# Four-layer mixture-of-experts kernel: gates of the first mixture broadcast by DMA, experts summed on GpSimd, routing steps in later places

## The reference, cut to what matters

```
# end of layer 1, dense mixture of 4 experts, every token goes through all four
gw  = softmax(h @ w_moe_gate.T)                # 4 gates of a token
hid = silu(h @ w1[e].T + b1[e])                # 128 -> 512, for each e
x   = x + sum_e gw[e] * (hid @ w2[e].T + b2[e])
# layer 2, one of 8 experts of a token
probs = softmax(layernorm(x) @ gate_w.T)
top   = max(probs); top_val = top / (top + 1e-8); expert = argmax(probs)
out   = layernorm(expert_ffn(...) * top_val)
```

## Time and profile before

| | |
|---|---|
| median of 3 runs | 1566.64 us |
| profiled execution | 1570.3 us, its span 1568.1 us |
| mixture stage, from its first instruction to the next stage's | about 474.5 to 958.2 us |
| PE / PEld busy | 84% / 65% of the span |
| DVE / ACT / POOL busy | 68% / 47% / 44% of the span |
| granted TensorE clock | 0.941 over the span |

### The profile page before, as it was taken

How to read it: one execution, slowest core, us unless ns; L and a number is a source line. 1 busy time by engine, 2 the same in 40 slices (tenths; PEclk the granted TensorE clock), 3 DMA queues, 4 the chain that set the end, 5 groups by cost and what they waited for, 6 DMA issues and landing times. The chain is left out here.

```text
span 1568.1 us, 33973 instructions
## 1 busy us (share of the span) xinstructions
PE 1310.5 (84%) x10546; PEld 1014.7 (65%) x10546; DVE 1063.9 (68%) x3597; ACT 743.8 (47%) x1503; POOL 694.1 (44%) x845
## 2 busy tenths in 40 slices
PE   3899999999875999999999964674787887829996
PEld 1566666666644888888888853564555655629996
DVE  3677777777646788888888863565588788722221
ACT  2345454545324676666666632453333333315553
POOL 2344444444320244545353542234366666525665
PEclk9899999999967999999999986998899999959998
DMA  2231212222102000000000004564211111259881
GB/s 79 29 41 26 36 27 33 29 31 31 17 1 81 3 14 8 14 7 14 7 12 9 11 11 123 167 178 118 72 52 46 46 51 45 40 189 312 261 266 40
DMA packets 61575, 100.97 MB, mean 64 GB/s; under 512 B 9698, under 2 KB 36331, under 8 KB 61120
## 3 DMA queue, kind: packets, MB, share of 16 engines
q1 hardware_dynamic: 51648, 78.58, 19.5%
q0 software_dynamic: 9856, 21.52, 4.4%
HBM read 62.96 MB, written 29.75 MB: 59 GB/s over the span
## 5 line engine op out<-in xcount | busy, mean ns | idle before, releaser
L1137 DVE TENSOR_TENSOR m_Sl<-m_S,m_Sh 128x512 fp32r<-128x512 f32 x256 | 174.8, 692 | 32.5 <-ACT m_S L1049 27.6
L1049 ACT ACTIVATE m_S<-PS,W 128x512 f32<-128x512 f32 x256 | 175.6, 686 | 33.4 <-PE PS L957 30.2
L1403 POOL DMA_INDIRECT rows<-r_row,r_posi x128 | 143.0, 1117 | 35.6 <-issue 35.6
L1389 POOL TENSOR_TENSOR r_soft<-r_euler,r_soft 128x32 f32<-128x32 f32 x16 | 86.9, 5429 | 132.5 <-DVE r_soft L1287 132.5
L1044 ACT ACTIVATE m_Sh<-PS,W 128x512 fp32r<-128x512 f32 x128 | 88.2, 689 | 106.2 <-PE PS L957 105.0
L750 DVE TENSOR_TENSOR am<-PS,C 128x512 f32<-128x512 f32 x192 | 119.4, 677 | 19.9 <-PE PS L442 19.9
L955 PE MATMUL PS<-m_HH,m_w1h 128*128 128x512 f32 x256 | 110.7, 432 | 14.5 <-DVE m_HL L1101 14.3
L1608 PEld LDWEIGHTS PS<-f_wt,f_hid 128*128 128x128 f32 x960 | 119.5, 192 | 4.2
L1608 PE MATMUL PS<-f_wt,f_hid 128*128 128x128 f32 x960 | 119.9, 275 | 0.0
L1597 PE MATMUL PS<-f_xT,f_wt 128*128 128x256 f32 x480 | 119.9, 387 | 0.0
L343 POOL TENSOR_TENSOR am<-am,C 128x512 f32<-128x512 f32 x64 | 81.4, 1272 | 80.2 <-ACT am L623 80.2
(11 more groups left out here) (242 smaller groups left out, 3242.5 us busy)
## 6 DMA issues: line engine op xcount, KB each, us to landing
f_wt<-wr SPq DMA_DIRECT2D x40, 578.0 KB
f_row<-rows SPq DMA_DIRECT2D x40, 260.0 KB
f_wt<-wr SPq DMA_DIRECT2D x40, 256.0 KB, 2.8
f_row<-rows SPq DMA_DIRECT2D x40, 132.0 KB, 2.1
mid<-f_res SPq DMA_DIRECT2D x40, 128.0 KB, 2.6
rows<-r_padding SPq DMA_DIRECT2D x16, 260.0 KB
X<-x SPq DMA_DIRECT2D x16, 256.0 KB, 5.5
qr<-qphi SPq DMA_DIRECT2D x64, 64.0 KB
```

Source lines behind the costliest of these rows:

```text
L1049: nc.scalar.activation(S[:, n % 3, :], PS[:, n % 3, :], ACT.Silu, bias=w("b1")[:, n:n + 1]).then_inc(s_ready, 1)
L1137: nc.vector.tensor_tensor(Sl[:, n % 4, :], S[:, n % 3, :], Sh[:, n % 4, :].bitcast(F32), ALU.subtract).then_inc(sl_ready, 1)
L1403: nc.gpsimd.indirect_dma_start(out=self.rows, out_offset=bass.IndirectOffsetOnAxis(ap=self.posi[:, u, t:t + 1], axis=0), in_=self.row[:, u ...
```

## The change

The gates are no longer spread over the partitions by PE. They are transposed once (2 transposes), written to a small DRAM tensor, and SP loads for each batch the 4 x 512 gates into all 128 partitions by one DMA with a repeated source (1 MB in SBUF), into one of two buffers. `gated` writes each expert to its own buffer (five in all), POOL adds them up in three 128x512 additions (`sums`), and PE transposes only the sum. `ROUNDED` becomes `(3,)`: ACT now writes `Sh` in three of four places. The first weights `w1` are loaded into `raw1` at the end of the front; weights are split one expert at a time, the high half on ACT, the low half on DVE, most of it inside batch 0. The router's steps of a batch move to the turn after, in other places, with two row buffers. Its exp becomes two Silus on ACT: e^y = -silu(y)/silu(-y). The count-dependent padding is issued half by SP and half by ACT, in the second router too. `sel` leaves the constants (256 KB).

```diff
@@ mixture, SP
-            sp.dma_start(raw1[:, :], w1t).then_inc(w1_in, 16)
-            sp.dma_start(raw2[:, :], w2t).then_inc(w2_in, 16)
+            for q in range(MOE):
+                sp.dma_start(raw2[:, q * SEQ:(q + 1) * SEQ], w2t[:, q * SEQ:(q + 1) * SEQ]).then_inc(w2_in[q], 16)
+            sp.wait_ge(gT_ready, 1)
+            sp.dma_start(gates_dram.rearrange("(h e) t p -> (e t) h p", h=2), gT[:, :, :]).then_inc(gates_out, 16)
+            sp.wait_ge(gates_out, 16)
+
+            def one(b, v, p, r, tp, tr):
+                if b is not None:
+                    if isinstance(b, int) and b == 1:
+                        sp.wait_ge(w_split, 2 * MOE)
+                    if not isinstance(b, int) or b >= 2:
+                        sp.wait_ge(oe_ready, MOE * (b + (-1)))
+                    src = gates_dram[:, bass.ds(b * CT, CT), :].rearrange("e t p -> e (t p)").unsqueeze(0)
+                    sp.dma_start(gb[v][:, :, :], src.to_broadcast([P, MOE, SEQ])).then_inc(gb_in[v], 16)
+            over_batches(sp, one)
             routing.sp_padding(sp)
@@ mixture, POOL
+            def sums(b, e, v):
+
+                pool.wait_ge(oe_ready, MOE * b + e + 1)
+                if e > 1:
+                    pool.wait_ge(summed, 3 * b + e - 1)
+                acc = oe[:, total_of(v), :]
+                nc.gpsimd.tensor_tensor(acc, acc, oe[:, e, :], ALU.add).then_inc(summed, 1)
+
+            def one(b, v, p, r, tp, tr):
+                if p is not None:
+                    sums(p, 2, 1 - v)
+                    sums(p, 3, 1 - v)
+                route(routing.pool_inverse_deviation, pool, p, 1 - v, tp)
+                if b is not None:
+                    sums(b, 1, v)
+                route(routing.pool_scatter, pool, r, v, tr)
@@ mixture, PE
+            def back(b, v):
+
+                pe.wait_ge(summed, 3 * b + 3)
+                after_previous(pe, x_ready, b)
                 for t in range(CT):
+                    mm = nc.tensor.transpose(PS[:, 7, t * P:(t + 1) * P], oe[:, total_of(v), t * P:(t + 1) * P], ident)
                 mm.then_inc(back_psum, 1)
...
                     lagging = chunk(b, p, n, 3)
                     if lagging:
                         down(*lagging)
+                    if n == 0:
+                        route(routing.pe_turn, pe, r, v, tr)
+                    if n == 3:
+                        route(routing.pe_scores, pe, r, v, tr)
+                    if n == 7 and p is not None:
+                        back(p, 1 - v)
+                    if n == 8:
+                        route(routing.pe_count, pe, r, v, tr)
@@ mixture, DVE
                     if n % 4 == 3:
                         lagging = chunk(b, p, n, 7)
                         if lagging:
+                            gated(lagging[0], lagging[1] // 4, v if n >= 7 else 1 - v)
+                    if n == 3:
+                        route(routing.dve_largest, dve, r, v, tr)
+                    if n == 4 and more:
+                        split_first(b + 1, 1 - v)
+                    if n == 5:
+                        route(routing.dve_pick, dve, r, v, tr)
+                    if n == 6 and more:
+                        split_second(b + 1, 1 - v)
+                    if n == 8 and p is not None:
+                        residual(p)
+                    if n == 9:
+                        route(routing.dve_statistics, dve, p, 1 - v, tp)
+                    if n == 10:
+                        route(routing.dve_place, dve, r, v, tr)
+                    if n == 12:
+                        route(routing.dve_gate, dve, r, v, tr)
+                    if n == 13:
+                        route(routing.dve_normalise, dve, p, 1 - v, tp)
@@ Routing
+    def act_exp(self, act, b, u, turn):
+
+        act.wait_ge(self.soft_ready, b + 1)
+        self.nc.scalar.activation(self.soft[:, 1, :, :], self.soft[:, 0, :, :], ACT.Silu)
+        self.nc.scalar.activation(self.soft[:, 2, :, :], self.soft[:, 0, :, :], ACT.Silu, scale=-1.0).then_inc(self.exp_ready, 1)
```

More of the change, by code:

```diff
@@ L942, in _ @@
         def _(pe):
-            pe.wait_ge(w_split, 3)
+            first = lambda b: isinstance(b, int) and b == 0
             def up(b, v, n):
@@ L948, in up @@
                     pe.wait_ge(parts, 2 * b + 2)
+                if first(b) and n % MOE_CHUNKS == 0:
+                    pe.wait_ge(w_split, 2 * (n // MOE_CHUNKS) + 1)
                 if n >= 3:
@@ L965, in down @@
                 f = slice(n * P, (n + 1) * P)
+                if first(b) and k == 0:
+                    pe.wait_ge(w_split, 2 * e + 2)
                 wait_high(pe, b, n)
@@ L985, in back @@
                 mm.then_inc(back_psum, 1)
-            def gates(b):
-                pe.wait_ge(gp_ready, b + 1)
-                after_previous(pe, gb_ready, b, MOE)
-                for t in range(CT):
-                    mm = nc.tensor.transpose(PS[0:2 * MOE, 6, t * P:(t + 1) * P],
-                                             gp[:, t * 2 * MOE:(t + 1) * 2 * MOE], ident)
-                mm.then_inc(gT_psum, 1)
-            def spread(b, e):
-                pe.wait_ge(gT_ready, b + 1)
-                if e:
-                    pe.wait_ge(gb_ready, MOE * b + e)
-                nc.tensor.matmul(PS[:, 6, :], selr[:, e * P:(e + 1) * P], gT[:, :], start=True,
-                                 stop=True).then_inc(gb_psum, 1)
@@ L1003, in _, with gates, one @@
-            beside = {11: routing.pe_turn, 13: routing.pe_scores}
-            def one(b, v, p, r):
+            def gates():
+                pe.wait_ge(gates_ready, 1)
+                for h in range(2):
+                    mm = nc.tensor.transpose(PS[:, 6, h * P:(h + 1) * P],
+                                             gate[:, 2 * h:2 * h + 2, :].rearrange("p e t -> p (e t)"), ident)
+                mm.then_inc(gT_psum, 1)
+            def one(b, v, p, r, tp, tr):
                 for n in range(N):
-                    if n == 0:
-                        route(routing.pe_count, pe, r)
@@ L1009, in one @@
                     if b is not None:
                         up(b, v, n)
-                        if n == 2:
-                            if isinstance(b, int) and b == 0:
-                                pe.wait_ge(w_split, 5)
-                            gates(b)
-                        if n in SPREAD:
-                            spread(b, SPREAD.index(n))
+                        if first(b) and n == 2:
+                            gates()
                     lagging = chunk(b, p, n, 3)
@@ new lines, in _, with gated @@
+            low(raw2, w2h, w2l, 0, 1)
+            routing.dve_begin(dve)
+            def gated(b, e, v):
+                dve.wait_ge(out_psum, MOE * b + e + 1)
+                if e == 0:
+                    dve.wait_ge(gb_in[v], 8 * (b + (2 - v)) if isinstance(b, int) else 8 * b + 8 * (2 - v))
+                    if not isinstance(b, int) or b >= 2:
+                        dve.wait_ge(back_psum, b + (-1))
+                elif not isinstance(b, int) or b:
+                    dve.wait_ge(summed, 3 * (b + (-1)) + e)
+                nc.vector.scalar_tensor_tensor(oe[:, e if e else total_of(v), :], PS[:, 3 + e % 2, :], w("b2")[:, e:e + 1],
+                                               gb[v][:, e, :], ALU.add, ALU.mult).then_inc(oe_ready, 1)
@@ L2004, in f, with pick @@
                 return [stats, normalise]
+            def pick(dve, b, u, turn):
+                routing.dve_largest(dve, b, u, turn)
+                routing.dve_pick(dve, b, u, turn)
             def a(b, u, nxt, sent):
```

247 lines of the change are left out of this document (114 added, 133 removed).

## The result

| | median us | range us | to the kernel before (95%) |
|---|---|---|---|
| before, beside it on the same chip | 1567.64 | 1566.07 to 1569.03 | |
| changed | 1539.71 | 1538.19 to 1540.69 | 0.982 (0.980 to 0.984) |

The kernel is 27.9 us faster, 1.8%. Forecast were 54.4 us (1512, range 1498 to 1535): the sign is right, the size is half, and the time lies outside the range.

What follows compares the result with a forecast made beforehand. PE's instruction count was taken to bound the stage. 40.4 - 9 (stalls) + 11.0 (start) + 2.0 - 1.0 (batch 0) + 8.8 (end) + 1.5 (second padding) + 0.7 (constants) = 54.4 us gained: median 1512 us, range 1498 to 1535.

Steps and rivals of the forecast that it cites:

- batches 0 to 15 (40.4 - 9 + 2.0 - 1.0): Batches: 40.4 us less PE work, 9 of stalls from sums, batch 0 2.0 shorter, 1.0 off for late gates.
- second padding: Second router's 8 padding issues split over two queues: 1.5 us gained (0 to 4), DMA engines being 84% busy there.
- the sums' price: Steady batches: POOL's sums hold up DVE's two-SBUF-input operations, new PE stall 0.6 us a batch, 9 us in all.
- 2.5 us of slack: Steady batches: `Sl` wanted 4.7 us after its `up`, comes after 2.1; uneven places take 1.1, POOL waits most of the rest.
- The router's steps are only moved: PE, each batch: 2.69 us of instructions removed, 24.4 us left; the router's steps change place only.
- where DVE is early: Sums of experts 3 and 2 fall at n = 0 to 4, in slack; expert 1's takes about 1.0 us of slack.
- DVE becomes the bound: Rival, steady batches: all sums cost DVE full time, 26.1 us a batch with waits, 1529 us; chance 0.20.
- My own sign: Whole prediction: it is wrong if PE's gaps add up to more than 20 us.
- `gated` comes first: End, last matmul to normalise of batch 15: `gated` ahead of the gate step, 7.1 us in place of 9.1, 2.0 gained.
- The scatter is late next: of those 4.0 us I count 3.4: End of stage: padding issued on two queues takes 4.2 us in place of 8.41; 3.4 us gained before the scatter limits.
- The exp's term: End of stage: gate step no longer waits 3.68 us for POOL's exp; less 0.2 for the longer gate, 3.4 us gained.
- the 25 at which it would set the pace: Rival: the gates' broadcast DMA bounds the stage from 25 us each, kernel slower from 28.6; chance 0.04.

Runs made afterwards that it cites:

- sums of one column: Changed kernel with POOL's three sums a batch adding one column in place of 512, waits and signals kept: 1513.0 us, period 24.34 us.
- the order of the buffers alone: Changed kernel with chunk 15 given buffer 1 of the three PSUM banks and S buffers, so two chunks at least lie between uses: 1529.1 us, period 25.60.
- padding-on-SP: Changed kernel with all 8 paddings of each router issued on SP's queue again, none on ACT's: 1535.3 us.
- SP-waits: Changed kernel with SP in place of POOL waiting for the last scatters' landing, in both routers: 1534.5 us.
- the run with quarters: Changed kernel with each of POOL's sums made as four instructions of 128 columns in place of one of 512: 1536.8 us, period 25.90.

## Why the prediction was wrong

Forecast were 54.4 us, the profiled executions differ by 30.3. By the terms of the sum:

| term | forecast | measured |
|---|---|---|
| start of the stage (forecast for the constants alone) | 0.7 | 1.45, of it 0.2 by the constants |
| PE's first matmul | 11.0 | 11.0 |
| batches 0 to 15 (40.4 - 9 + 2.0 - 1.0) | 32.4 | 20.1 |
| last matmul to the next stage | 8.8 | 0.1 |
| second padding | 1.5 | -0.6 |
| the stages between, untouched | 0 | -1.8 |

**The failed step: the sums' price.** "I take 0.6 us a batch of new stall on PE" was the term that carried the miss. Measured is 1.68 (26.02 - 24.34) in each steady batch. It sets in with batch 4: batches 1 to 3 take 22.7, 24.3 and 24.8 us, with sums of one column 22.7, 24.3 and 24.3. From the first matmul of batch 1 to the last of batch 15 the changed kernel takes 387.2 us and the one with sums of one column 365.9: the sums cost 21.3 us where I had 9. Without them the forecast of these batches was 367.4 us (407.8 - 40.4), so PE's own work was right to 1.5 us. Of the 12.3 us that the row of batches falls short, 10.7 are in these fifteen and 1.5 in batch 0. The bound from both sides held (0 to 3.8 us for DVE, 2.4 measured), and so did DVE's own 21.9 (21.8).

What failed is how much of DVE's stretch the slack takes. I counted 2.5 us of slack from the written distance of `up` to its `Sl`, and overlooked three things. The distance isn't 3 places everywhere: at the turn of the batch the rings of three leave one (removing that gives 0.4 us a batch). "The router's steps are only moved" was wrong: the turn at n = 0 now waits for a normalise at n = 13, with two places between them (0.6 us in the trace, 0.3 when it is moved). And the sums don't lie where I put them. I gave expert 1's the 1.0 us and took the other two for nearly free, "where DVE is early". Expert 2's stands on POOL behind a scatter (issued until 711.05, the sum starts at 711.08), meets an `Sl` and is the dearest, 1.3 us; beside expert 3's stands the routing's subtraction, 0.76 us. How much of each PE feels was not tried apart.

The time per batch is that of my rival "DVE becomes the bound": its 26.1 us came out as 26.02. I gave it 0.20. In part that is luck: it had 25.7 us of DVE work and 0.4 of waits, measured are 24.2 and 1.8, and the order of the buffers alone, with DVE's work unchanged, gave back 0.4 us. So DVE's queue is what PE follows, but not by its length alone. My own sign, PE's gaps adding up to more than 20 us, did not fire: in the second stretch above they are 388.20 - 374.23 = 14.0 us. A late weight load (PEld) isn't a gap of PE, and PE's durations are modelled; the distances between starts give the 21.3.

**Batch 0.** It took 26.2 us where it took 25.7, 0.5 lost in place of 1.0 gained (2.0 - 1.0). DVE stood 2.9 us for the gates and PE 1.4; the load of the gates took 8.0 us. I had 4.9 for it, from a row that I called "alone", though SP issued the second megabyte at 474.95, 0.4 us behind it. Why the 2.0 us of fewer instructions didn't show was not tried.

**The end: two steps.** "`gated` comes first" was right, but the sums it feeds stand on POOL behind the scatter of batch 13, which ends at 891.92; 0.9 us lost in place of 2.0 gained. "The scatter is late next: of those 4.0 us I count 3.4" was wrong in kind. The view of SP's waits in the kernel before already had 1.6 us for another engine behind the paddings, which I did not read: POOL, whose drain of 5.3 us follows the scatter's landing, was already last (it reached the barrier at 956.8, SP at 955.3), so nothing was to be gained by faster padding, and the faster padding delayed the scatter by 2.4 us. The padding-on-SP and SP-waits runs show both halves. The exp's term was right: 3.4 us.

**The second padding.** The same: 0.6 us lost; 0.7 came back with the padding on SP alone.

**Not the change's doing.** Between the two padding parts nothing was edited. That stretch took 426.35 us before (959.52 to the paddings) and 428.2 here, and 425.3 to 427.8 in the eleven runs of the experiments with the same code in it: it varies by that much. The same holds for the start of the stage. DVE's first use of the constants comes at 7.57 us in place of 7.77, so they gave 0.2 us of the 0.7; the rest of the 1.45 is within the 6 us by which the end of the front varies.

**What was right.** PE's first matmul to 0.1 us, PE's own work in a batch (24.4, measured 24.34), and that the gates would come a little late. The broadcast takes 7.9 us from issue to landing, far from the 25 at which it would set the pace. The Trainium skill, page "GPSIMD Engine Reference", section "Key points", had named two SBUF inputs or a 2-port mode as what contends with POOL; the trace agrees for two inputs, and my error was in taking the warning as a small number.

## What to carry to other kernels

Work moved from a bound engine to POOL can be paid by DVE, where DVE has operations with two SBUF inputs beside it. Here 4.2 us a batch of POOL's sums (1.66, 1.28 and 1.30) made DVE's queue 2.4 us longer, and with DVE busy for 93% PE felt 1.7 us of it, more than the 1.4 us that the move had saved PE. So price each such operation from a row of one beside POOL, and where the other queue is nearly full, count the stretch as lost and not as hidden. Before counting slack, find the shortest distance in each ring of buffers, at the turn of the loop too. At a stage's end read who the barrier waits for in the kernel before; the last queue to issue need not be the last to arrive.

## What the runs showed of the hardware

- A DVE operation of 32 columns with two SBUF inputs takes 0.19 us apart and, in the steady batches, 0.87 to 0.95 beside a 128x512 addition on POOL, and ends 0.05 us behind it. (At the end of the stage one that began while a scatter was being issued, 0.62 us ahead of an addition, took 1.95.) Beside an addition of 128 columns the routing's product takes 0.49. So the way is held for one POOL instruction at a time.
- A 128x512 subtraction with two SBUF inputs (`Sl`), begun 0.17 us ahead of the addition, took 2.0 us in place of 0.69 and ended 0.56 us behind it. Another, begun 0.16 us ahead, kept its 0.68 us, and the addition took 1.66 in place of 1.28. What decides between the two was not tried.
- Casts with one SBUF input are held too: the split's took 0.68 us in place of 0.42 in the run with quarters, and a cast of 4 columns took 0.65 beside the last sum (0.17 apart). The searches (MAX8) and the reciprocal of 32 columns kept their 0.15 and 0.35 us beside the sums. So it is not only the number of inputs in SBUF that decides; which form of cast is held was not tried.
- POOL's closing drain, begun behind the landing of the scatters, took 5.29 us at the end of the mixture and 2.36 at the end of the softmax attention, before, after, and with the padding on SP. Begun while the scatters were still issued (SP waits), it ended 6.1 us behind the end of the last issue. Why the two stages differ was not tried.
- At the end of the mixture the last indirect scatter landed 2.5 to 2.6 us after the start of its issue with one queue of paddings beside it (before, padding on SP), and 4.2 to 4.9 us with two (the changed kernel and the other ten). At the second router it took 4.3 us with one queue (before) and 5.4 with two (changed).
- Some 18 us into batch 0 PE stands 1 to 2 us. Behind that the granted clock fell to its 1.2 GHz level in two of the twelve profiled executions of the changed kernel and the experiments (waits of 1.88, and of 1.46 and 0.70 us) and stayed at 1.00 in the other ten (first waits of 1.0 to 1.5 us); batch 0 took 28.0 us with the fall and 25.7 to 27.3 without.
